# Gate-times-up product and row moves ahead of the state-times-C product on GpSimd, in a one-core selective scan with a mixture of experts

## What is computed

```python
# branch s: selective scan, 128 channels, 64 states each
left, right = split(y @ W_up + b_up)
u = silu(conv3(left))
delta = softplus(u @ W_delta + b_delta)
Bm, Cm = u @ W_B, u @ W_C
h[t] = exp(delta[t] * A) * h[t-1] + (delta[t] * u[t]) * Bm[t]
left[t] = sum_over_states(h[t] * Cm[t]) + u[t] * D
s = xn + (left * silu(right)) @ W_down + b_down
# branch moe: top 2 of 8 experts, hidden width 1024
g, up = xn @ w1[e], xn @ w3[e]
moe = sum over the two chosen e of weight * ((silu(g) * up) @ w2[e])
```

## Time and profile before

| what | us |
|---|---|
| median of 3 runs (lowest, highest) | 1514.64 (1512.84, 1518.68) |
| the profiled execution | 1516.97 |
| its span, first to last instruction | 1515.0 |
| TensorE busy with matmuls | 1263.9 (83%) |
| VectorE busy | 1199.2 (79%) |
| GpSimd busy | 1121.9 (74%) |
| ScalarE busy | 749.4 (49%) |

### The profile page before, as it was taken

One profiled execution on the slowest core, in us unless ns is written; L12 is line 12 of the kernel. 1 busy time (PEld: TensorE's weight loads), 2 busy tenths in 40 slices (PEclk: granted clock), 3 DMA queues, 4 the chain that ended last, 5 costly groups with the idle time before them and its releaser, 6 DMA issues. The chain is left out here.

```text
span 1515.0 us, 21600 instructions
## 1 busy us (share of the span) xinstructions
PE 1263.9 (83%) x5800; PEld 915.9 (60%) x5800; DVE 1199.2 (79%) x1618; ACT 749.4 (49%) x1613; POOL 1121.9 (74%) x1090
## 2 busy tenths in 40 slices
PE   5847789989898999999999999987989799897720
PEld 5635357767676666666766667665767566675410
DVE  6746678978798788978887898777887688797738
ACT  1443564547454745456454655464546355355511
POOL 0265387879888787879887878787877778789853
PEclk7578999999999999999999999999999999996555
DMA  7012435446544564565374456335633554563336
GB/s 218 30 35 59 146 136 166 127 118 205 151 138 119 167 180 133 148 178 154 123 201 122 140 167 204 111 106 180 172 121 109 182 162 136 162 190 116 99 125 218
DMA packets 124963, 218.02 MB, mean 144 GB/s; under 512 B 15264, under 2 KB 40992, under 8 KB 124832
## 3 DMA queue, kind: packets, MB, share of 16 engines
q10 hardware_dynamic: 73728, 134.25, 30.8%
q1 hardware_dynamic: 43616, 61.82, 12.7%
q0 software_dynamic: 7488, 20.46, 4.3%
HBM read 191.57 MB, written 24.90 MB: 143 GB/s over the span
## 5 line engine op out<-in xcount | busy, mean ns | idle before, releaser
L409 POOL TENSOR_TENSOR arena<-arena,c_rep 128x512 f32<-128x512 f32 x512 | 602.7, 1183 | 193.3 <-DVE arena L937 186.8
L937 DVE TENSOR_TENSOR_SCAN arena<-bank,carry,arena 128x512 f32<-128x512 f32 x512 | 652.2, 1274 | 31.1 <-ACT bank L708 30.7
L1171 PE MATMUL bank<-xgT,wring 128*128 128x256 f32 x2240 | 537.4, 383 | 19.7 <-DMA wring<-in_w_all 6.8
L1171 PEld LDWEIGHTS bank<-xgT,wring 128*128 128x128 f32 x2240 | 430.1, 192 | 83.0 <-issue 17.6
L708 ACT ACTIVATE bank<-arena,a_neg 128x512 f32<-128x512 f32 x512 | 354.9, 693 | 94.2 <-ACT bank L708 47.7
L928 DVE TENSOR_TENSOR arena<-bank,b_rep 128x512 f32<-128x512 f32 x512 | 351.4, 686 | 38.5 <-PE bank L1184 18.2
L636 ACT ACTIVATE th<-bank 128x256 f32<-128x256 f32 x312 | 119.7, 384 | 457.1 <-PE bank L1171 432.2
L1140 PE MATMUL bank<-wring,hid 128*128 128x256 f32 x1120 | 300.5, 391 | 32.3 <-ACT o_sb L647 27.8
L1184 PE MATMUL bank<-stack,pick 128*128 128x512 f32 x512 | 278.1, 566 | 19.4 <-DVE arena L928 19.4
L1140 PEld LDWEIGHTS bank<-wring,hid 128*128 128x128 f32 x1120 | 206.1, 191 | 136.8 <-issue 90.0
L949 DVE SCALAR_TENSOR_TENSOR gt<-th,bank 128x256 f32<-128x256 f32 x312 | 127.6, 409 | 178.3 <-ACT th L636 111.9
(11 more groups left out here) (167 smaller groups left out, 850.4 us busy)
## 6 DMA issues: line engine op xcount, KB each, us to landing
arena<-delta_d ACTq DMA_DIRECT2D x512, 256.0 KB, 3.7
wring<-in_w_all SPq DMA_DIRECT2D x64, 384.0 KB, 4.2
arena<-results SPq DMA_DIRECT2D x16, 512.0 KB, 6.0
xn<-in_x SPq DMA_DIRECT2D x4, 1024.0 KB, 9.6
xn_d<-xn SPq DMA_DIRECT2D x4, 1024.0 KB, 5.9
parts_d<-spare SPq DMA_DIRECT2D x16, 256.0 KB, 3.8
stack<-parts_d SPq DMA_DIRECT2D x16, 256.0 KB, 5.4
out<-arena SPq DMA_DIRECT2D x8, 512.0 KB, 3.2
```

Of the source, the lines that this page charges most:

```text
L409: pool.tensor_tensor(p_ring[:, s % P_RING, :], h_ring[:, s % H_RING, :], of_chunk(c_rep, c, 2), ALU.mult).then_inc(s_hc, 1)
L937: v.tensor_tensor_scan(out=h_ring[:, s % H_RING, :], data0=a_bank[s % 2][:, :], data1=b_ring[:, s % B_RING, :], initial=carry[:, q:q + 1], ...
L1171: ins = pe.matmul(bank[:, m * SLOT:(m + 1) * SLOT], wring[:, kk, (2 * m + h) * P:(2 * m + h + 1) * P], xgT[:, i % 2, h, :], start=(h == 0) ...
```

## The change

In GpSimd's loop over the pairs two lines trade places. For the pairs 0 to 510 the turn's work (hidden product, scatter, gather) now stands ahead of the same pair's product of state and C. For the last pair, whose two calls stand behind the loop, the order stays. Nothing is added or removed.

```diff
             for s in range(PAIR_COUNT):
                 if s:
+                    after_turns(BY_PAIR[s - 1])
                     state_by_c(s - 1)
-                    after_turns(BY_PAIR[s - 1])
                 for b in batches_at(s):
                     values_of_halves(b)
```

## The result

| | before | after |
|---|---|---|
| median | 1514.57 us (1512.84 to 1518.68) | 1548.01 us (1547.18 to 1551.06) |
| ratio | | 1.022, 95% interval 1.0195 to 1.0246 |
| span of the profiled execution | 1515.0 us | 1545.1 us |

The change costs 33 us by the medians.

A forecast was written before the change was run, and what follows sets the result against it. TensorE, then ScalarE, then VectorE was taken to bound the kernel. Late sums of quads +20 us, less 6 us from the earlier hidden product, make +14 us on 1514.6 us: 1528.6 us, range 1512 to 1541 us.

The forecast's parts named there:

- What bounds the kernel: Main stretch: TensorE sets the pace, then ScalarE, then VectorE; GpSimd follows; TensorE busy 91 of 100 us.
- Waits change sides: On GpSimd, hidden product's gate waits grow from 38 to some 190 us; product's scan waits fall from 187 to under 20.
- The stops: At the sums of quads TensorE waits for late products of state and C: 24.8 us added over 27 late quads.
- three groups: Quads by last pair's turn: gather or scatter, 14 short, 16.6 us; plain step, 6, 4.6 us; no GpSimd work, 9, 6.1 us.
- the larger part: Scatter and gather, moved ahead with the hidden product, were named the larger cost: 16.6 us at 21 quads ending with them.
- The clock: Rival, chance 0.07: TensorE's granted clock falls with its pauses; five extra slow stretches make +15 us, 1544 us.
- The forecast's own sign for this rival: The falling clock would show as a granted clock lower than 0.98 in the stretches from 200 to 1300 us.
- How much reaches the end, 0.83: Behind late sums: share of tanhs finding ScalarE idle for TensorE, times 24.8 us, gives 20.5 us; 20 taken, bounds 8.4 to 24.8.
- the rival "absorbed": TensorE's pauses at sums replace ones it has anyway, or GpSimd catches up: +2.4 us, 1517 us; chance 0.20.
- The gain: Earlier hidden product saves 4 us of TensorE waits in the main stretch, 2 us among empty tiles: 6 us, bounds 0 to 10.
- The sum in its new form: The forecast's own sum over the profiled span: +20 us from late sums less 6 us gained, +14 us, with no clock term.

The follow-up runs named there:

- the second profile: The changed kernel, unaltered, run and profiled once more; median 1543.7 us, against 1515.1 us for the kernel before, ratio 1.0183.
- the run with pair 131 put back: The changed kernel with the old order at one pair of 512, pair 131, the last of quad 32; median 1539.1 us.

## Why the prediction was right or wrong

**What bounds the kernel: right.** TensorE sets the pace; nearly all of its stops at the sums appear in the time of everything behind.

**Waits change sides: right.** Forecast 190 us in about 140 cases for the gate; measured 202.6 us in 140. The product's wait for the scan fell to 46 us, not under 20 us; the cause of that isn't shown.

**The stops: right in number, 10% low in sum.** Forecast 27 late quads and 24.8 us added; measured 28 stops (8 before) and 27.3 us added. (The forecast's three groups have 29 quads, 14, 6 and 9, not 27.) At quad 89 it was 1.66 for 1.67 us, at quad 22 1.68 for 1.4 us. Carrying one engine's queue forward in its new order, against the recorded starts of the others, is a reckoning that held. Two places were taken wrongly. The sum of a chunk's first quad waits at L1116, ahead of L1118, so the margin of quad 32 is 0.95 us less than I took (474.88 and not 475.83 us). And the last quad, left out because its own order stays, stood 3.0 us where it had stood 1.8 us, since the pairs ahead of it hand on their delay.

**Which part is to blame: right for the places, wrong for the parts.** Quads that end with a scatter or a gather have 15 of the stops and 18.0 of the 27.3 us, where the forecast had 14 and 16.6 us, and adding both to the hidden product alone costs 22 us (1526.2 to 1548.0). But I read from this that they are the larger part by themselves. Alone they cost no time (-7 us): it takes both delays to pass the margin.

**The clock, put at nothing: wrong, the largest step that failed.** The sum had no term for it, and the rival was given a chance of 0.07 as something apart. It belongs to the stops: 20.5 us more at the lower clock, all of it within or behind stops, worth 10 to 11 us (10 us more at the lower clock were 5.5 us between the two profiles). In the second profile it was 10 us more and 5 us of time, and in the run with pair 131 put back nothing more, with 36.1 us of stops. So the stops make room for it, and how much comes differs by execution. The forecast's own sign for this rival, a granted clock under 0.98 from 200 to 1300 us, was too coarse: it reads 0.98 in both profiles and 0.99 before. The Trainium skill, TensorE: Matmul & The Clock Gate, section HAM oscillation, describes a kernel in which waits for DMA send TensorE's clock back down again and again. The trace agrees that the clock falls at pauses, with 0.54 in the stretch behind the stop of 2.19 us, and shows beside it that the same stop can also pass without.

**How much reaches the end, 0.83: wrong, the second step that failed.** I multiplied by the share of tanhs that found ScalarE idle. That share counts pairs; it doesn't say how much of a stop the pairs behind take back. What is taken back shows in TensorE's waits for VectorE at the spreads, 19.4 to 16.9 us. So the rival "absorbed" is right for 2.5 us and no more, and 27.3 - 2.5 = 25 us reach the end, where the forecast had 20 us: 5 us of the miss. The run with pair 131 put back is the cleanest case, since its lower clock is as long as before (34.1 us): from pair 16 to 484 it added 24.4 us of stops and took 20.8 us more.

**The gain: too high.** TensorE's waits for the hidden product fell by 3.1 us in the main stretch (4.4 to 1.3 us) and by 9.9 us among the empty tiles. From pair 484 to the last, though, it took 75.7 us before and 74.6 us after: 1 us, where the waits alone would promise ten. GpSimd is the bound there, as the forecast had it; other waits took their place, TensorE's for `o_sb` among them (9.8 us at the dummy products). So 3 + 1 = 4 us and not 6.

**The sum in its new form.** From pair 16 to 484: stops +26, clock +11, hidden product -3, waits for VectorE at the spreads -2.6 makes +31 us, for 31.6 us measured. In the second profile it is 26 + 5.5 - 3 - 2.6 = 26 us, for 26.1 us. In the run with pair 131 put back it is 24.4 - 3 - 2.6 = 19 us, for 20.8 us; 2 us stay open there. The difference between the two medians of the changed kernel, 1548.0 and 1543.7 us in two sets of runs, is about what the clock makes between the two profiles; that the clock is its cause isn't shown.

## What to carry to other kernels

Two pieces of work that trade places on an in-order engine take their whole tail along, DMA issues too. Ask at each consumer by how much the later one still comes in time: delays that cost little or nothing alone (-7 and +10 us here) can cost 33 us together, once they pass the margin. Where a consumer stands too early in the pacing engine's queue, moving it one step back was worth more (19 us) than any order of the producer, until the ring of buffers became the next wait (two steps: +23 us). And a stop of the engine that sets the pace should be counted nearly whole (25 of 27 us here), with a bound of its own for its clock (0 to 11 us here).

## What was unexpected of the hardware

The same kernel, with the same stop of 2.19 us at the same place, was followed by 6 us of work at the lower clock in one execution (0.54 granted from 480 to 487 us) and by none in another (1.00). At quads 96, 102 and 112 the lower clock stood behind the stop in two executions and not in a third with nearly the same stops. Over the whole scan it made 5.5 us between two profiles of the same kernel.
